# Four one-element products against one product of four elements: the key scales of a delta-rule attention kernel

## The reference, cut to what matters

```python
q = causal_conv_silu(x @ Wq.T, conv_q)      # k and v alike
beta = jax.nn.sigmoid(x @ Wb.T)             # one number per token and head
q = l2norm(q) * hd ** (-0.5)
k = l2norm(k)                               # x * rsqrt(sum(x*x) + 1e-6)
def step(state, inp):
    qt, kt, vt, bt = inp
    pred = jnp.einsum('bhd,bhdv->bhv', kt, state)
    delta = bt[..., None] * (vt - pred)
    state = state + jnp.einsum('bhd,bhv->bhdv', kt, delta)
    ot = jnp.einsum('bhd,bhdv->bhv', qt, state)
    return (state, ot)
```

## Time and profile before

| what | value |
|---|---|
| median of 3 runs | 1777.48 us (1776.48 to 1781.47) |
| the profiled execution, its own time | 1781.47 us |
| its span in the profile | 1779.7 us |
| granted TensorE clock, mean | 0.979 |
| busy: TensorE, VectorE, ScalarE, GpSimd | 95%, 83%, 68%, 62% |
| the chain that ended last | TensorE 84%, VectorE 8%, ScalarE 5% |
| the stretch of the 64 units | 206 to 1305 us, granted clock 1.00 |

### The profile page before, as it was taken

How to read it: one execution, slowest core, us unless ns; L and a number is a source line. 1 busy time by engine, 2 the same in 40 slices (tenths; PEclk the granted TensorE clock), 3 DMA queues, 4 the chain that set the end, 5 groups by cost and what they waited for, 6 DMA issues and landing times.

```text
span 1779.7 us, 41654 instructions
## 1 busy us (share of the span) xinstructions
PE 1692.1 (95%) x14070; PEld 1247.5 (70%) x14070; DVE 1470.7 (83%) x3684; ACT 1206.8 (68%) x2911; POOL 1104.7 (62%) x1148
## 2 busy tenths in 40 slices
PE   7999899999999999999999999999988788888888
PEld 5577567777777777777777777777767566666667
DVE  5322599999999999999999999999986788888863
ACT  2134477777777777777777777877754588778763
POOL 1600067777777777776666666666666478778841
PEclk9999999999999999999999999999986699999999
DMA  9433310111110110100001000101002000000033
GB/s 313 148 96 110 105 31 22 38 31 27 36 33 27 30 36 21 39 18 27 27 18 27 24 18 24 30 12 30 15 2 60 1 1 1 2 1 1 1 89 91
DMA packets 66098, 73.85 MB, mean 41 GB/s; under 512 B 10975, under 2 KB 54767, under 8 KB 65775
## 3 DMA queue, kind: packets, MB, share of 16 engines
q1 hardware_dynamic: 62919, 63.92, 12.2%
q0 software_dynamic: 3072, 8.65, 1.5%
HBM read 55.45 MB, written 17.10 MB: 41 GB/s over the span
## 4 chain that ended last, share of the span: by engine, by line
PE 84%; DVE 8%; ACT 5%; issue 1%; POOL 1%; SPq 0%; DMA 0%; POOLq 0%; DVEq 0%; ACTq 0%
PE banks L735 19%; PE banks L893 6%; PE banks L762 4%; PE banks L849 3%; PE banks L770 3%; PE banks L868 3%; PE banks L778 3%; PE banks L700 3%; PE banks L807 3%; PE banks L815 2%; PE banks L821 2%; PE banks L949 2%; PE banks L814 2%; PE banks L1025 2%; PE banks L719 2%; PE banks L960 2%
## 5 line engine op out<-in xcount | busy, mean ns | idle before, releaser
L735 PE MATMUL banks<-xnT,hw 128*128 128x512 f32 x768 | 414.1, 622 | 2.5 <-DVE cv L2034 2.5
L2090 DVE CAST_PREDICATED MM<-lmask,banks 128x512 bf16<-128x512 uint32 x384 | 272.5, 710 | 35.8 <-PE banks L815 31.5
L2034 DVE SCALAR_TENSOR_TENSOR cv<-banks,hc,cv 128x510 f32<-128x510 f32 (+2 forms) x384 | 284.8, 742 | 5.5 <-ACT cv L1439 0.8
L1503 ACT ACTIVATE T<-banks 128x256 bf16<-128x256 f32 x384 | 149.3, 389 | 147.4 <-PE banks L807 147.1
L2694 POOL TENSOR_TENSOR X<-X,yrow 128x512 f32<-128x512 f32 x128 | 163.3, 1276 | 66.3 <-ACT yrow L1535 66.3
L2658 POOL TENSOR_TENSOR kn<-nsum,half_pos 128x4 f32<-128x4 f32 x64 | 65.6, 1025 | 142.2 <-DVE nsum L2059 142.2
L815 PEld LDWEIGHTS banks<-MM,T 128*128 128x128 bf16 x1536 | 104.3, 98 | 65.4 <-issue 48.4
L814 PEld LDWEIGHTS banks<-T,MM 128*128 128x128 bf16 x1280 | 99.1, 97 | 65.3 <-ACT T L1503 63.1
L2034 DVE SCALAR_TENSOR_TENSOR cv<-banks,hcv,cv 128x510 f32<-128x510 f32 (+2 forms) x192 | 141.4, 736 | 1.4 <-ACT cv L1439 1.3
L893 PE MATMUL banks<-ho,OT 128*128 128x256 f32 x512 | 141.7, 400 | 0.0
L807 PEld LDWEIGHTS banks<-MM,Gb 128*128 128x128 bf16 x1536 | 84.2, 98 | 81.3 <-issue 43.7
(11 more groups left out here) (318 smaller groups left out, 4885.9 us busy)
## 6 DMA issues: line engine op xcount, KB each, us to landing
MM<-in_eye SPq DMA_DIRECT2D x64, 256.0 KB, 2.7
slot_rows<-zeros SPq DMA_DIRECT2D x1, 5304.0 KB, 20.1
xs<-slot_rows SPq DMA_DIRECT2D x13, 408.0 KB, 4.0
slot_out<-ye SPq DMA_DIRECT2D x13, 384.0 KB, 2.7
hw<-in_hw SPq DMA_DIRECT2D x16, 256.0 KB, 3.4
wT<-in_winit SPq DMA_DIRECT2D x8, 384.0 KB, 3.9
wgu<-in_wgu SPq DMA_DIRECT2D x1, 2816.0 KB
w1c<-in_ew SPq DMA_DIRECT2D x16, 176.0 KB
```

The source lines that it names most:

```text
L735: ins = pe.matmul(PROJ[t][:], hw[:, kk, t, :], xnT[:, kk, u.b * BLK:(u.b + 1) * BLK], start=(kk == 0), stop=(kk == KD - 1))
L1503: act.activation(strips(T1[:].rearrange("p i t -> p (i t)"), LEVELS[lv], 0, 1), grams_bank(u)[:, 0:TILES * 64].rearrange("p (k e) -> p k e ...
L2034: dve.scalar_tensor_tensor(o, y, taps_of(t)[:, TAPS - 1 - i:TAPS - i], o, ALU.mult, ALU.add).then_inc(dve_conv, 1)
L2090: dve.copy_predicated(dst, m, ps).then_inc(dve_mm, 1)
```

## The change

In `key_scales` four `tensor_scalar` operations, each of one element per partition with `beta` as the scalar of each partition, are replaced by one `tensor_tensor` over four elements per partition. The four values of `beta` lie apart in `sig0` (one column of each tile), so they are read with a stride. The wait in front and the semaphore increment behind stay as they are.

```diff
             def key_scales(u):
                 beta = sig0[:, u.b * TPB:(u.b + 1) * TPB, bass.ds(u.h, 1)].rearrange("p c o -> p (c o)")
                 dve.wait_ge(dve_scale, 3 * u.n + 2)
-                for i in range(TPB):
-                    last = dve.tensor_scalar(ksc[:, u.b % 2, i:i + 1], kinv[:, i:i + 1], beta[:, i:i + 1], None, ALU.mult)
-                last.then_inc(dve_scale, 1)
+                dve.tensor_tensor(ksc[:, u.b % 2], kinv[:], beta, ALU.mult).then_inc(dve_scale, 1)
```

## The result

| | kernel before | changed kernel |
|---|---|---|
| first comparison, median | 1776.98 us (4 runs, 1768.19 to 1781.47) | 1790.03 us (the first 4 runs, 1789.05 to 1796.13); 1795.5 us (all 35 on record, 1787.0 to 1798.6) |
| ratio, first comparison | | 1.0096, 95% interval 1.0066 to 1.0125 |
| second comparison (below), median | 1780.5 us (29 runs) | 1801.79 us (6 runs) |
| ratio, second comparison | | 1.0133, 95% interval 1.0096 to 1.0171 |
| span of the profiled execution | 1779.7 us | 1800.7 us |

The account below looks back on a forecast made before the run. TensorE was taken to set the pace, with VectorE close behind. About 0.34 us lost per unit over the 64 units, 21.1 us in sum, on 1777.5 us gave 1798.6, say 1799 us; range 1789 to 1809.

Parts of the forecast that it names:

- 0.03 us to spare for VectorE at L821: In each unit TensorE's L821 is about 0.03 us from waiting for VectorE's residual, so delays pass nearly whole.
- The product is held by mask until its end: In `key_scales` the new product waits for GpSimd's `mask` and takes 0.94 us, making `refine` 0.37 us late.
- The sum: Units 3 to 63 and unit 2 lose 0.34 us each, unit 63 0.37, units 0 and 1 nothing: 21.1 us.
- the release after mask: The held product was to end 0.04 us after GpSimd's `mask` ends.
- The fill: Units 0 and 1, where the pipeline fills: between -0.40 and +0.45 us each, taken as 0.
- L807 was to be some 0.12 us late: TensorE's L807, which needs `invert(u2,5)`, has 0.25 us of cover, so it starts some 0.12 us late.
- the signs forecast for the profile: Product about 0.94 us, L821 and L807 idle about 20 us together, units 17.75 us apart, TensorE busy time about the same.
- GpSimd's next operation can't take the turn: After `mask`, GpSimd's L2685 needs `refine`, so it isn't ready and can't hold VectorE next.
- rival three: Held, and dearer: GpSimd's delayed followers cost each unit some 0.2 us more, 12 us: 1811 us; chance 0.04.
- Rival four: Held, but partly absorbed: only L807 is late, 0.12 us per unit, 7 us: 1785 us; chance 0.04.
- Rival one: The product isn't held; VectorE's saving becomes idle time, only fill and last unit gain about 1 us: 1776.5; chance 0.09.
- Rival two: Faster: VectorE's 0.40 us comes through in every unit, 26 us, 1752 us; chance 0.03.

Follow-up runs that it names:

- second comparison: The changed kernel unaltered, timed again against the kernel before with more runs: medians 21.3 us apart, ratio 1.0133.
- Eight one-element operations: The kernel before with four more one-element products, into a spare tile, ahead of the four in `key_scales`: ratio 1.0158, stretch 28.9 us longer.

## Why the prediction was right

*TensorE bounds the stretch, with 0.03 us to spare for VectorE at L821.* Shown. Eight one-element operations delivered 0.46 of 0.49 us; giving VectorE 0.3 us and more per unit back (PSUM operand, mask moved) gained nothing, because VectorE then waits for TensorE: `refine` 0.18 us for L821, and the later L821 doesn't start earlier though its residual is done.

*The product is held by mask until its end.* Shown, from four sides: with mask elsewhere 158 ns, with a PSUM operand 154, with mask in halves 391, and unchanged 926. The Trainium skill has this in "SBUF — State Buffer", section "Who interferes with whom": a VectorE instruction with two SBUF inputs contends with a GpSimd instruction that reads SBUF, and the second to issue fully blocks until the first finishes. For a product (`mask`) on GpSimd's side the runs agree, down to one element on VectorE's (146 ns in the median of all, 0.95 us for the first of each four). On GpSimd's side they don't quite: the power reads SBUF too, and beside it VectorE's product took 0.16 to 0.17 us.

*The sum.* Forecast 21.1 us; the stretch says 20.4, the spans 21.0, the second comparison 21.3, the first 13 us by the medians. Against the first median, 1790.03 us, the forecast of 1799 is 9 us high; against the median of all 35 it is 3.5 us high. Of the terms, the release after mask was mis-sized: 0.04 us taken, 0.02 measured, so 0.34 per unit became 0.32. The start of `refine`, forecast 0.86 us after the product's, is 0.87 in unit 29 and 0.84 in the mean of units 3 to 61. The fill was mis-sized the other way: units 0 and 1 were taken at 0 and unit 2 at 0.34. Unit 0 was not held (0.17 us), but units 1 and 2 were, for 1.12 and 1.16 us, and the first three intervals are together 1.0 us longer than before. So two small errors in part offset each other, and the sum is closer than its terms. L807 was to be some 0.12 us late: it starts 1.00 us after L735 where it was 0.86, so 0.14. Two of the signs forecast for the profile came out otherwise: the waits of the two weight loads grew by 19.5 and 8.8 us, 28 and not 20 together, since part of L807's was covered; and TensorE's busy time was not about the same but grew with the stretch (1091 of 1099 us before, 1106 of 1115 after), as the modelled ends fill the gaps.

*GpSimd's next operation can't take the turn.* Shown in the timeline: L2683 comes at 722.53, after a wait of 0.43 us for `refine`. That its followers would cost more (rival three) didn't come true: GpSimd's delays end in its idle time, and the stretch holds no more than the direct loss. Rival four, that only L807 would count (7 us), is excluded by the row of L821 and by the 20 us.

*Rival one, not held.* Excluded by the row of L2068. *Rival two, faster.* It had been priced at 26 us; the run with the PSUM operand, which has the saving without the hold, is at 0.9993 (0.9971 to 1.0016).

## What to carry to other kernels

Fewer operations on VectorE are no gain by themselves when another engine sets the pace; first look for the idle time that would take the saving up, and for the distance to the next instruction of the pacing engine, since a delay goes through where a saving does not. Before an operation is merged or rewritten, look at where its inputs lie and at what GpSimd runs at that moment: in this kernel a product that reads a second tensor from SBUF took 0.9 us beside a GpSimd product of 1.27 us (so did a `tensor_scalar` over four elements), 0.16 us with GpSimd's operation moved and 0.39 with it cut in two. An operation over four elements with one input in PSUM took 0.15 beside it. The sign is in the trace of the kernel before: operations of one form whose median is far above their minimum (151/500/575 ns in the earlier trace rows), with a GpSimd operation that ends just ahead of theirs.

## What the runs showed that I had not expected

A power on GpSimd (1.03 us over four elements, both inputs in SBUF) did not hold a VectorE product with two SBUF inputs, wherever in its duration the product began: 0.07 us behind the power's start (unit 0, 0.17 us), 0.41 (L2238, 0.69 us, its shortest) or 0.74 (unit 2, 0.16 us). The elementwise product on GpSimd did in every unit from 1 on. A power over more elements was not tried, and what sets the two apart stays open.

Four one-element `tensor_tensor` follow each other more closely than four one-element `tensor_scalar` with a scalar per partition: once the first is through, three take 0.21 us together against 0.37, and each stands in the profile with 146 ns instead of 205.

The time from the start to the first `key_norms` scattered between 200.5 and 213.8 us over the profiled executions of kernels that are alike up to there, while the stretch of the 64 units repeated to within 0.5 us for the changed kernel (1114.0 and 1113.5). A change in one stretch of a long kernel can be sized far more closely by that stretch than by the kernel's time. What makes the early part scatter was not looked into.
